# A new order on TensorE for the fourth QKV tile, the probability transposes and the values

## What is computed

```python
def _L0_attn_ref(x, wqkv, wo, q_norm_w, k_norm_w):
    qkv = jnp.einsum('btc,oc->bto', x, wqkv)
    q, k, v = (to_heads(t) for t in jnp.split(qkv, 3, axis=-1))
    q, k = _rope(_rmsnorm(q, q_norm_w), cos, sin), _rope(_rmsnorm(k, k_norm_w), cos, sin)
    attn = jnp.einsum('bhtd,bhsd->bhts', q, k) * D ** (-0.5)
    attn = jax.nn.softmax(jnp.where(causal, attn, -jnp.inf), axis=-1)
    out = jnp.einsum('bhts,bhsd->bhtd', attn, v)
    return jnp.einsum('bte,ce->btc', out.transpose(0, 2, 1, 3).reshape(B, T, H * D), wo)

def _L0_ffn_ref(x, gate_w, expert_w):
    chosen = jnp.argmax(jnp.einsum('bsh,eh->bse', x, gate_w), axis=-1)
    onehot = jax.nn.one_hot(chosen, gate_w.shape[0], dtype=x.dtype)
    return x + jnp.einsum('bsef,bse->bsf', jnp.einsum('bsh,efh->bsef', x, expert_w), onehot)

xn = _layernorm(x)
return x + _L0_attn_ref(xn, ...) + _L0_ffn_ref(xn, gate_w, expert_w)
```

## Time and profile before

| | |
|---|---|
| median of 3 runs | 2036.11 us (2035.03 to 2037.41) |
| the profiled execution | 2035.76 us |
| its span | 2033.9 us |
| TensorE busy | 97% |
| VectorE busy | 86% |
| ScalarE busy | 79% |
| GpSimd busy | 68% |

### The profile page before, as it was taken

One profiled execution on the slowest core, in us unless ns is written; L12 is line 12 of the kernel. 1 busy time (PEld: TensorE's weight loads), 2 busy tenths in 40 slices (PEclk: granted clock), 3 DMA queues, 4 the chain that ended last, 5 costly groups with the idle time before them and its releaser, 6 DMA issues.

```text
span 2033.9 us, 48319 instructions
## 1 busy us (share of the span) xinstructions
PE 1966.9 (97%) x16520; PEld 1642.1 (81%) x16520; DVE 1741.2 (86%) x4144; ACT 1607.6 (79%) x5095; POOL 1377.0 (68%) x1975
## 2 busy tenths in 40 slices
PE   4899999999999999999999999999999999999997
PEld 4777888888888888888888888888888888888885
DVE  5799888888888888888988889889888888888875
ACT  3787788888788788787878878878888887888775
POOL 6567766577666767658766686666876677766764
PEclk8999999999999999999999999999999999999999
DMA  5111211112211132111221122221222112222244
GB/s 188 58 48 40 68 48 61 61 45 77 92 61 48 46 102 79 54 58 59 73 94 48 48 79 73 74 63 53 64 74 84 48 53 84 69 68 64 82 133 148
DMA packets 84548, 145.81 MB, mean 72 GB/s; under 512 B 9808, under 2 KB 63184, under 8 KB 84176
## 3 DMA queue, kind: packets, MB, share of 16 engines
q1 hardware_dynamic: 78160, 125.93, 19.3%
q0 software_dynamic: 6144, 16.79, 2.5%
HBM read 102.05 MB, written 40.63 MB: 70 GB/s over the span
## 4 chain that ended last, share of the span: by engine, by line
PE 82%; POOL 6%; DVE 5%; ACT 4%; issue 2%; DMA 0%; POOLq 0%; DVEq 0%
PE ps_g L737 36%; PE ps_g L834 14%; PE ps_s L823 11%; PE ps_g L843 11%; PE ps_g L799 5%; PE ps_s L816 3%; POOL rms_inv L526 2%; POOL qk_rot L520 2%; ACT prob L618 2%; POOL qk_rot L531 2%; PE ps_g L764 1%; DVE qk_sin L1013 1%; DVE qk_cos L1013 1%; PE ps_g L746 1%; ACT qk_sq L602 1%
## 5 line engine op out<-in xcount | busy, mean ns | idle before, releaser
L520 POOL TENSOR_TENSOR qk_rot<-qk_cos,qk_sin 128x128 f32<-128x128 f32 x1024 | 466.6, 477 | 577.6 <-DVE qk_sin L1013 572.3
L737 PE MATMUL ps_g<-w_qkv,xn_t 128*128 128x384 f32 (+1 forms) x3072 | 640.2, 351 | 2.3 <-DVE xn_t L928 1.5
L618 ACT ACTIVATE prob<-ps_s,neg_max 128x256 f32<-128x256 f32 (+3 forms) x1024 | 536.3, 550 | 0.3 <-DVE neg_max L1027 0.3
L737 PEld LDWEIGHTS ps_g<-w_qkv,xn_t 128*128 128x128 f32 x3072 | 526.6, 190 | 5.5 <-issue 2.2
L526 POOL TENSOR_TENSOR rms_inv<-ss,neg_half 128x8 f32<-128x8 f32 x256 | 448.6, 1752 | 0.0
L1027 DVE TENSOR_REDUCE neg_max<-ps_s 128x2 f32<-128x512 f32 (+3 forms) x512 | 404.8, 810 | 0.0
L628 ACT ACTIVATE prob_t<-ps_g 128x512 f32<-128x512 f32 (+2 forms) x768 | 370.1, 526 | 37.5 <-PE ps_g L834 37.5
L834 PE MATMUL ps_g<-ident,prob 128*128 128x128 f32 x2560 | 361.7, 278 | 3.9 <-DVE prob L1038 1.6
L834 PEld LDWEIGHTS ps_g<-ident,prob 128*128 128x128 f32 x2560 | 290.3, 141 | 74.3 <-DVE prob L1038 45.1
L531 POOL TENSOR_TENSOR qk_rot<-qk_rot,rms_inv 128x256 f32<-128x256 f32 x512 | 324.1, 654 | 20.1
L843 PE MATMUL ps_g<-prob_t,v 128*64 128x512 f32 (+3 forms) x2048 | 305.6, 441 | 1.0 <-ACT prob_t L628 1.0
(11 more groups left out here) (108 smaller groups left out, 2517.8 us busy)
## 6 DMA issues: line engine op xcount, KB each, us to landing
w_tile<-w_dram SPq DMA_DIRECT2D x120, 512.0 KB, 3.5
x_rows_s<-x_dram SPq DMA_DIRECT2D x120, 128.0 KB, 2.1
y_dram<-y_rows_s SPq DMA_DIRECT2D x120, 128.0 KB, 1.7
xin<-in_x SPq DMA_DIRECT2D x16, 512.0 KB, 4.2
out<-acc SPq DMA_DIRECT2D x15, 512.0 KB, 3.3
w_dram<-w_tile SPq DMA_DIRECT2D x8, 512.0 KB, 3.0
x_dram<-xn SPq DMA_DIRECT2D x2, 1920.0 KB, 18.0
y_back<-in_expert_t SPq DMA_DIRECT2D x8, 256.0 KB, 3.7
```

Source lines behind the costliest of these rows:

```text
L520: r = pool.tensor_tensor(rot[:, :, a, :], cos[:, :, a, :], sin[:, :, 1 - a, :], ALU.add)
L618: r = act.activation(prob[:, h, prob_at(k):prob_at(k) + w], ps_s[n % 2][:, h, 0:w], ACT.Exp, bias=neg_max[:, i, h:h + 1], scale=1.0, accum ...
L737: r = pe.matmul(ps, lhs(a, c), rhs(b, c), start=(c == parts[0] and (a, b) == TERMS[0]), stop=(c == parts[-1] and (a, b) == TERMS[-1]))
```

## The change

On TensorE, the transposes of the sorted rows and the fourth QKV tile go ahead of the transposes of the third and fourth items' probabilities. Behind those come the expert's product, or the projection in a unit without a tile, then the values, then the second visit of the scores. The list of bank uses and ScalarE's order follow; VectorE's, GpSimd's and SP's orders are as before.

```diff
             tiles = sorted_tiles(u)
-            if live(u - 1):
-                found += ["pt2.0", "pt2.1", "pt3.0"]
             found += [f"xs{i}" for i in tiles[0:2]]
             if live(u + 1):
                 found += ["qkv3"]
             if live(u - 1):
+                found += ["pt2.0", "pt2.1", "pt3.0"]
+            found += [f"ex{i}" for i in tiles[0:1]] + [f"xs{i}" for i in tiles[2:3]]
+            if projection(u) and not tiles:
+                found += ["proj"]
+            if live(u - 1):
                 found += ["o"]
-            found += [f"ex{i}" for i in tiles[0:1]] + [f"xs{i}" for i in tiles[2:3]]
             found += [f"ex{i}" for i in tiles[1:3]]
             if turns_x(u):
                 found += ["xt0", "xt1"]
-            if projection(u):
+            if projection(u) and tiles:
                 found += ["proj"]
...
             def unit(u):
                 tiles = sorted_tiles(u)
-                if live(u - 1):
-                    take_pt(u - 1, 2)
-                    take_pt(u - 1, 3)
                 for i in tiles[0:2]:
                     take_xs(u, i)
                 if live(u + 1):
                     take_qkv(u + 1, 3)
+                if live(u - 1):
+                    take_pt(u - 1, 2)
+                    take_pt(u - 1, 3)
                 if live(u):
                     softmax(u, 0)
                     softmax(u, 1)
-                if live(u - 1):
-                    take_o(u - 1)
...
                 for i in tiles[2:3]:
                     take_xs(u, i)
+                if live(u - 1):
+                    take_o(u - 1)
                 if live(u):
                     scale_probs(u, 0)
...
                 if live(u):
                     scores(u, 0)
-                if live(u - 1):
-                    transpose_probs(u - 1, 2)
-                    transpose_probs(u - 1, 3)
                 for i in tiles[0:2]:
                     transpose_xs(u, i)
                 if live(u + 1):
                     qkv(u + 1, 3)
                 if live(u - 1):
-                    values(u - 1)
+                    transpose_probs(u - 1, 2)
+                    transpose_probs(u - 1, 3)
                 for i in tiles[0:1]:
                     expert(u, i)
                 for i in tiles[2:3]:
                     transpose_xs(u, i)
+                if projection(u) and not tiles:
+                    project(u)
+                if live(u - 1):
+                    values(u - 1)
                 if live(u):
                     scores(u, 2)
                 for i in tiles[1:3]:
                     expert(u, i)
                 if turns_x(u):
                     transpose_xn(batch_of(u) + 1)
-                if projection(u):
+                if projection(u) and tiles:
                     project(u)
```

## The result

| | before | after |
|---|---|---|
| median | 2035.57 us (4 runs) | 2176.59 us (4 runs, 2174.25 to 2178.06) |
| ratio | 1 | 1.069, interval 1.0677 to 1.0703 |
| span of the profiled execution | 2033.9 us | 2172.4 us |

The change costs 141 us. The forecast was 2173. The kernel before took 2035.3 us beside the first four experiments and 2037.9 beside the last four, so across them the ratios are what to compare. Lines of the changed kernel stand two to four lower than before: 737 is 739, 799 is 801, 816 is 818, 823 is 825, 834 is 836, 843 is 845, 985 is 989, 1013 is 1017, 1055 is 1059. The experiments that add lines move them once more: in the run with other banks 739 is 745, 836 is 842 and 630 is 636; with the values first 739 is 743, 836 is 840, 845 is 849, 989 is 995 and 1017 is 1023.

What follows compares the result with a forecast made beforehand. TensorE's own queue was taken to bound the kernel (busy 97%), with the new order adding stalls on bank releases. 2035.8 + 120.6 (units with a tile) + 17.0 (without) = 2173 us; own range 2140 to 2205, later given as 2135 to 2205.

Steps and rivals of the forecast that it cites:

- The ties: PSUM banks: each group waits for the release four places ahead; three stalls (0.2, 0.5, 0.5 us), +1.21 us per tile unit.
- its anchor of VectorE's queue: VectorE's queue hangs on TensorE's q/k transposes; products of tile 2 end at 1025.39, tile 3's at 1028.53, in unit 64.
- 108 units with a tile: Units with a tile and a following unit: 1.21 us each, 130.7, less give-backs of 8.4 and about 1.7; sum 120.6 us.
- units 3 to 8: Units without a tile, with weight splitting on VectorE: 6 x 1.6, less some waits for GpSimd, 8.8 us.
- nine others without a tile: Later second visit (+0.46) and qkv0 stalled behind the projection's release (+0.45): 9 units x 0.91 = 8.2 us.
- units 1, 2 and 9: Units without a tile whose wait for GpSimd at line 799 hides the loss: 0.
- The give-back at line 799: In units % 8 = 1 TensorE's wait for GpSimd goes: 14 units give back 0.6 us each (8.4).
- A: Rival: only the expert's operand counts, its matmul waits for line 985 alone; +0.46 per unit, 50 us, 2090; 7%.
- B: Rival: faster; both listed waits (45.1 and 14.8 us) go and VectorE's work isn't late; 1976 us; 4%.
- C: Rival: the banks don't hold and no wait was there; the reorder is neutral, 2036 us; 2%.
- E: Rival from the experiments: VectorE's whole queue is the bound, whatever the banks; 2176 us with other banks; no chance given.
- D: Rival: stalls make TensorE's clock fall; +20 us in the 16 units without a tile, +150 in all; 5% for over 30 us.

Runs made afterwards that it cites:

- the run with other banks: Changed kernel, same order, with the list of bank uses dealt out again in units with one tile: 2122.29 us, ratio to before 1.0427.
- the values first: Changed kernel with the values ahead of the expert's matmul again in units with a tile: 2209.0 us, ratio 1.0846.
- the rows-first run: Changed kernel with VectorE taking the sorted rows (line 989) ahead of the two row maxima: 2211.24 us, ratio 1.0869.
- The extra pass: One more VectorE pass over 256 columns ahead of tile 3's products: changed kernel 2219.97 us, ratio 1.0909; kernel before, ratio 1.0016.

## Why the prediction was right, point by point

**The new order's gains.** The 45.1 us of waits for line 1038 were read as no wait, for scores and next group overlap by 0.07 us at both places. In after they overlap by 0.07 still, with the rows' transposes there, which don't need the probabilities: the scores start at 1096.02 for 1.30, the transposes at 1097.25. From the last score matmul's start to the next group's, the step costs 0.32 us behind scores over 512 columns and 0.20 behind those over 128, whatever follows. The Trainium skill's sentence that a change of tiling mode drains TensorE (TensorEngine Tiling, Key Properties) fits: no record of these two kernels has it cheaper.

**The ties and their times.** In unit 64, behind the first visit:

| | forecast | measured |
|---|---|---|
| qkv3 starts | 1.83 | 1.83 |
| line 989 ends | 4.17 | 4.17 |
| products of tile 3 end | 4.92 | 4.83 |
| expert's matmul starts | 4.97 | 4.98 |
| second visit | 8.22 | 8.16 |

The prediction called its anchor of VectorE's queue wrong if these products ended before 4.95. They did, but its own sum has them at 4.92, so that sign was set wrongly; the anchor itself, the end of tile 2's products, is 1.78 in both kernels. The products end 0.09 sooner than I had them, for VectorE saves the overlap of two adjoining passes as well as the idle 0.32, and the matmul starts 0.15 behind the release, not 0.05. The expert's matmul takes 0.88 to the values' start, not 0.95: the 0.04 that the sum added there for the step to 64-column products isn't seen. So a unit pays 1.14 to 1.15 us, not 1.21.

**The sum.** From the lengths of the units in the two traces:

| | forecast | measured |
|---|---|---|
| 108 units with a tile | 120.6 | 111.1 |
| units 3 to 8 | 8.8 | 16.9 |
| nine others without a tile | 8.2 | 13.0 |
| units 1, 2 and 9 | 0 | -2.4 |
| together | 137.6 | 138.6 |

That the total is within 1 us is luck: the mechanism was right, and the errors of the terms (-9.5, +8.1, +4.8 and -2.4 us) cancel. *The 108 units with a tile* pay 1.14 to 1.15 us instead of 1.21, which is 7 of the 9.5; a batch's first unit pays 0.3 less than others, as forecast (0.25), but unit 120 pays nothing, and units behind one without a tile pay 0.1 less. *Nine units without a tile:* 1.45 us each and not 0.91. Both stalls came as worked out, second visit at 8.56 (forecast 8.6) and qkv0 1.00 us late (1.79 us behind the q/k transposes for 0.79; forecast 0.9), in unit 28:

```profile
508.14 1.67 PE L739 MATMUL ps_g<-w_out,o_t 128*128 128x256 f32 x12 [1.06 <-DVE qk_sin L1017]
...
513.20 1.09 PE L801 MATMUL ps_g<-ident,qk_rot 128*128 128x128 f32 x8
514.99 1.32 PE L739 MATMUL ps_g<-w_qkv,xn_t 128*128 128x384 f32 x6 [0.70 <-DVE acc L1059]
```

but the next unit gives back only 0.1 of it (1.03 us longer instead of 1.15), not the half that I took: ScalarE's and VectorE's work behind qkv0 is as late as qkv0. *Units 3 to 8:* units 3 and 6 pay 4.1 and 5.4 us. In both TensorE idles over 2 us and the clock falls (below), which costs some 1.6 us: unit 3 is 1.57 us shorter with the values first, where its clock stayed. In unit 6 moreover a fourth tie of the list had escaped me: with xt0 and xt1 between, kt stands four places behind proj, and line 801 waits 2.26 us for line 1059. *Units 1 and 2:* the term was put at 0. TensorE's idle times did cancel as forecast (unit 1: 0.59 us for softmax and 2.70 for GpSimd before, 1.88 for line 1017 and 1.35 for GpSimd after), but the clock doesn't fall in them any more, 1.4 us each the other way; unit 9 pays 0.4.

**The give-back at line 799** in the units behind a batch's first was forecast at 0.6; it is 0.65 to 0.7 in every second of them, and 0.2 in the others, where VectorE adds the experts' rows too.

**The rivals.** A fell with the rows-first run, B and C with the result, E (named in the experiments only) with the other banks: the same queue of VectorE, and 54 us less. The extra pass (43 us in one kernel, 3 in the other) fits, but E had expected the 43 as well. D came true in two units and almost without effect on the sum, since two others no longer pay for it: the granted clock falls to half twice in each kernel behind the start, in units 1 and 2 before and 3 and 6 after. The windows of units 3, 4, 6 and 64 of after (us, busy times of PE, PEld, DVE, ACT, POOL, granted clock, DMA share, GB/s), to be read against the earlier trace rows:

```profile
84.58:103.35 18.77, 15.99 (x121) 12.67 (x120) 12.90 (x31) 12.49 (x41) 9.88 (x15) 0.91 0.13 43
103.35:120.35 17.00, 14.42 (x121) 11.85 (x120) 14.86 (x38) 12.43 (x40) 10.91 (x16) 1.00 0.14 47
137.37:158.37 21.00, 16.85 (x129) 14.24 (x129) 14.04 (x30) 14.02 (x44) 9.63 (x15) 0.92 0.12 39
1095.84:1112.13 16.29, 15.52 (x130) 12.76 (x130) 12.68 (x28) 12.40 (x39) 11.37 (x17) 1.00 0.20 66
```

**What stays open:** why units at u % 16 of 0 and 1 shift by 0.2 to 0.3 us when only units without a tile are changed, and why unit 120 differs from the other batches' first units; and the 0.57 us that the new order still costs with other banks, of which the trace shows who is waited for (ScalarE's copy of pt2.0) but no run took that away. The low end of the range stands in the prediction as 2140 and as 2135; both hold 2176.6.

## What to carry to other kernels

Where results rotate through a few banks, a group waits not only for its operands but for whoever reads the result that many places ahead of it; after each reordering, write the list out, put beside each place the time at which its bank's last reader ends, and look for the queue that is late there. A wait that the profile names may be a cost of the step itself: compare the same step at a place where nothing is waited for. And ask of a stall that you remove what is next: here the removal of a tie that cost 0.10 us won 0.02 to 0.04 in an ordinary unit, and that of three ties half of 1.15 us.

## What the runs showed of the hardware

In the changed kernel TensorE's granted clock fell to half in unit 3 behind an idle time of 2.09 us ahead of the projection, and in unit 6 behind one of 2.26. It stayed at 1.00 in unit 4 over 1.88 us, and in unit 8 over 2.12. With the values first it stayed at 1.00 in unit 3 too, over 2.10 us (the last line below). So the length of the idle time alone doesn't decide it.

```profile
90.27 2.28 PE L739 MATMUL ps_g<-w_out,o_t 128*128 128x256 f32 x12 [2.09 <-DVE qk_sin L1017]
...
108.84 1.67 PE L739 MATMUL ps_g<-w_out,o_t 128*128 128x256 f32 x12 [1.88 <-DVE qk_sin L1017]
...
151.27 1.06 PE L801 MATMUL ps_g<-ident,qk_rot 128*128 128x128 f32 x8 [2.26 <-DVE acc L1059]
...
181.47 1.66 PE L739 MATMUL ps_g<-w_out,o_t 128*128 128x256 f32 x12 [2.12 <-DVE qk_sin L1017]
...
91.40 1.64 PE L743 MATMUL ps_g<-w_out,o_t 128*128 128x256 f32 x12 [2.10 <-DVE qk_sin L1023]
```

The twelve matmuls of the projection took 2.28 us in unit 3 and 1.67 in unit 4. The stalls of 0.2 to 0.7 us, three in each unit with a tile, never brought the clock down: from unit 7 to unit 126 it doesn't fall.
